# A graph kernel's attention stage: destination terms expanded in bfloat16 parts, with another order of the engines' work

## The reference, cut to what matters

```python
es = jnp.einsum('nhd,hd->nh', x, a_s)
ed = jnp.einsum('nhd,hd->nh', x, a_d)
logit = jax.nn.leaky_relu(es[src] + ed[dst], NEG_SLOPE)
logit = jnp.where(mask[:, None], logit, -1e+30)
mx = jax.ops.segment_max(logit, dst, num_segments=N)
p = jnp.exp(logit - mx[dst]) * mask[:, None]
den = jax.ops.segment_sum(p, dst, num_segments=N)
alpha = p / jnp.where(den > 0, den, 1.0)[dst]
msg = alpha[..., None] * x[src]
out = jax.ops.segment_sum(msg, dst, num_segments=N)
```

## Time and profile before

| | |
|---|---|
| median of 3 runs | 6694.62 us (6692.63 to 6696.04) |
| the profiled execution | 6689.12 us |
| its span | 6686.9 us |
| PE / DVE / ACT / POOL busy | 3841.0 / 3444.8 / 898.4 / 4148.2 us |
| attention stage | from about 1518 to 3014 us of the span |
| table made (L800, 16 copies) | 1508.33 to 1517.89 us |

### The profile page before, as it was taken

One profiled execution on the slowest core, in us unless ns is written; L12 is line 12 of the kernel. 1 busy time (PEld: TensorE's weight loads), 2 busy tenths in 40 slices (PEclk: granted clock), 3 DMA queues, 4 the chain that ended last, 5 costly groups with the idle time before them and its releaser, 6 DMA issues. The chain is left out here.

```text
span 6686.9 us, 101415 instructions
## 1 busy us (share of the span) xinstructions
PE 3841.0 (57%) x17939; PEld 2899.4 (43%) x17940; DVE 3444.8 (52%) x10929; ACT 898.4 (13%) x2786; POOL 4148.2 (62%) x3995
## 2 busy tenths in 40 slices
PE   0332222215666666662467777777677777777766
PEld 0221111115666666661434444444444444444446
DVE  4632222214444444448955665656566566556654
ACT  0210000000000000003331111111111111111111
POOL 3067777764444443434228888888888888888870
PEclk9855555555555555555688888888888888888888
DMA  1355555533333333332268788787778877787874
GB/s 49 117 137 145 142 145 145 145 83 97 95 96 96 97 97 96 95 89 101 50 181 169 165 170 169 165 170 167 168 165 169 170 167 169 169 167 166 171 151 127
DMA packets 917009, 908.21 MB, mean 136 GB/s; under 512 B 231003, under 2 KB 735099, under 8 KB 916759
## 3 DMA queue, kind: packets, MB, share of 16 engines
q0 software_dynamic: 238848, 434.00, 32.4%
q1 hardware_dynamic: 678119, 473.77, 26.3%
HBM read 656.68 MB, written 250.64 MB: 136 GB/s over the span
## 5 line engine op out<-in xcount | busy, mean ns | idle before, releaser
L1409 POOL DMA_INDIRECT sums<-msg_bsum,msg_sidx x928 | 1558.8, 1680 | 308.0 <-issue 268.9
L1551 PEld LDWEIGHTS msg_fwd_ps<-msg_onehot,msg_hid 128*128 128x128 f32 x3712 | 639.8, 224 | 1422.1 <-issue 1313.4
L1418 POOL DMA_INDIRECT msg_ga<-ab,msg_idx x928 | 951.4, 1025 | 390.7 <-issue 240.8
L851 POOL TENSOR_SCALAR att_keyhot<-k_ramp,att_keys 128x128 f32<-128x128 f32 x1028 | 602.3, 604 | 895.9 <-PE att_sum_ps L949 873.4
L1564 PE MATMUL msg_pre_ps<-msg_rw,msg_lt 128*128 128x512 f32 x1856 | 1110.2, 684 | 37.1 <-DVE msg_xs L1488 28.1
L1551 PE MATMUL msg_fwd_ps<-msg_onehot,msg_hid 128*128 128x64 f32 x3712 | 621.6, 298 | 819.0 <-DVE l_fwd L1470 814.3
L686 POOL DMA_INDIRECT max_xe<-rows,max_idx x832 | 800.1, 962 | 422.8 <-issue 253.3
L949 PE MATMUL att_sum_ps<-att_px,att_keyhot 128*128 128x136 f32 x2056 | 559.1, 454 | 537.4 <-DVE l_acc L895 521.5
L949 PEld LDWEIGHTS att_sum_ps<-att_px,att_keyhot 128*128 128x128 f32 x2056 | 478.3, 331 | 563.7 <-DVE l_acc L895 546.8
L1553 PE MATMUL msg_bwd_ps<-msg_hid,msg_same 128*128 128x256 f32 x1856 | 708.9, 469 | 0.0
L1522 ACT ACTIVATE msg_bsum<-msg_bwd_ps 128x256 f32<-128x256 f32 x928 | 356.2, 384 | 2564.5 <-PE msg_bwd_ps L1553 2550.1
(11 more groups left out here) (260 smaller groups left out, 4807.6 us busy)
## 6 DMA issues: line engine op xcount, KB each, us to landing
msg_rw<-ab SPq DMA_DIRECT2D x928, 128.0 KB
att_xe<-xe SPq DMA_DIRECT2D x1028, 72.0 KB, 2.5
att_keyrow<-key SPq DMA_DIRECT2D x257, 256.0 KB, 3.5
xe<-max_xe SPq DMA_DIRECT2D x104, 576.0 KB, 3.5
msg_lt<-in_efT SPq DMA_DIRECT2D x928, 32.0 KB
msg_ga<-ab,msg_idx POOLq DMA_INDIRECT x928
sums<-msg_bsum,msg_sidx POOLq DMA_INDIRECT x928
rows<-node_rows SPq DMA_DIRECT2D x50, 288.0 KB, 2.4
```

What stands on the lines that cost most here:

```text
L851: pool.tensor_scalar(keyhot[:, b, u, :], K.ramp[:, 1:P + 1], keys[:, b, u:u + 1], None, ALU.is_equal).then_inc(s_kh, 1)
L1409: pool.indirect_dma_start(T.sums[u % 2], bass.IndirectOffsetOnAxis(ap=sidx[:, b, u:u + 1], axis=0), bsum[:, b, u, :], None, compute_op=ALU ...
L1418: pool.indirect_dma_start(ga[:, b, u, :], None, T.ab, bass.IndirectOffsetOnAxis(ap=idx[:, b, u:u + 1], axis=0)).then_inc(s_ga[b], 16)
L1551: pe.matmul(fwd_ps[u % 2][:, q * WIN:(q + 1) * WIN], hid[:, b % 2, u, HID + q * P:HID + (q + 1) * P], onehot[:, b, u, :], start=True, stop ...
```

## The change

In words:

1. `node_maxima` writes the table as three bfloat16 parts: the term rounded to bfloat16, the rest rounded again, and the rest of that. A column of the table has 48 bfloat16 numbers. For each part there is a cast of all 3200 numbers of a partition, a subtraction (not after the last), and sixteen copies into the table, a buffer of its own now.
2. `expand` is a bfloat16 matmul with 48 columns. DVE's `select` has a first step more (step -1): a reduction that adds the three parts out of PSUM into `dv`; the other steps read `dv`.
3. `spread` is ACT's: `away` = |part + 1 - keyrow|, then `keyT` = relu(1 - away), in bfloat16. It comes last in ACT's tick, after `exponentials`. ACT also issues the `keyrow` transfer, into two slots for four.
4. PE does `expand(t-1)` before `sums(t-3)`. DVE does `add`, `weigh(t-3)`, and then the steps of `select(t-2)` with an `add` between.
5. `px` has two slots for four. `expand` waits for the reduction of two groups earlier and no longer for the argument.
6. The tables `reg_w` and `reg_e` of the second layer are loaded in `edge_inputs` for `lists`.

The core of the diff:

```diff
@@ node_maxima
-            for q, r in quads:
-                out, src = to_keys(q, r)
-                dve.tensor_copy(out, src).then_inc(s_keyed, 1)
-            dve.wait_ge(s_keyed, len(quads))
+            all4 = "p t r s h -> p (t r s h)"
+            rest = both[:, :, :, :, :].rearrange(all4)
+            for i in range(TERMS):
+                part = term[:, :, :, :, :].rearrange(all4)
+                if i:
+                    dve.wait_ge(s_keyed, i * len(quads))
+                L.link(dve.tensor_copy(part, rest))
+                if i < TERMS - 1:
+                    L.mark(dve.tensor_tensor(rest, rest, part, ALU.subtract))
+                for q, r in quads:
+                    out, src = to_keys(q, r, i)
+                    dve.tensor_copy(out, src).then_inc(s_keyed, 1)
+                L.wait()
+            dve.wait_ge(s_keyed, TERMS * len(quads))
@@ relation_attention
-        keyT = ph.sb("keyT", [P, RG, U * P])
+        away = ph.sb("away", [P, U * P])
+        keyT = ph.sb("keyT", [P, RG, U * P], BF16)
+        dv = ph.sb("dv", [P, U, S2])
-        px = ph.sb("px", [P, RG, U, XR])
-        dst_ps = [ph.ps(f"dst_ps{b}", [P, U, S2]) for b in range(2)]
+        px = ph.sb("px", [P, 2, U, XR])
+        dst_ps = [ph.ps(f"dst_ps{b}", [P, U, TERMS * S2]) for b in range(2)]
...
             def select(j, b, step):
-                if step == 0:
+                if step == -1:
                     dve.wait_ge(s_dst, j + 1)
+                    dve.tensor_reduce(dv[:, :, :], dst_ps[b % 2][:, :, :].rearrange("p u (t c) -> p u c t", t=TERMS),
+                                      AX.X, ALU.add).then_inc(s_sc, 1)
...
@@ DVE's tick
-                    if has(2) and u < 3:
-                        select(t - 2, slot(2), u)
-                    if has(3) and u == 2:
+                    if has(3) and u == 0:
                         weigh(t - 3, slot(3))
-                if has(1):
-                    spread(t - 1, slot(1))
+                    if has(2):
+                        select(t - 2, slot(2), u - 1)
...
@@ ACT
-            pipeline(act, GROUPS, RG, [(0, keep), (2, exponentials)])
+            def load(j, b):
+                if past(j, 2):
+                    act.wait_ge(s_away, j - 1)
+                    settle(act, K)
+                act.dma_start(keyrow[:, b % 2, :], key[ds(j, 1), :].to_broadcast([P, U * P])).then_inc(s_kr[b % 2], 16)
+
+            def spread(j, b):
+                act.wait_ge(s_kr[b % 2], filled(j, b, 2, 16) if isinstance(j, int) else (j - b % 2) * 8 + 16)
+                if past(j, 1):
+                    act.wait_ge(s_kT, j)
+                act.activation(away[:, :], keyrow[:, b % 2, :], ACT.Abs, bias=K.part1[:, 0:1], scale=-1.0).then_inc(s_away, 1)
+                if past(j, RG):
+                    act.wait_ge(s_dst, j - RG + 1)
+                act.wait_ge(s_away, j + 1)
+                act.activation(keyT[:, b, :], away[:, :], ACT.Relu, bias=K.ones[:, 0:1], scale=-1.0).then_inc(s_kT, 1)
+
+            pipeline(act, GROUPS, RG, [(0, load), (0, keep), (2, exponentials), (1, spread)])
@@ PE
-            pipeline(pe, GROUPS, RG, [(3, sums), (1, expand)])
+            pipeline(pe, GROUPS, RG, [(1, expand), (3, sums)])
```

More of the change, by code:

```diff
@@ L36 @@
 KC = -(-STEPS // P)
+TERMS = 3
 KKC = -(-KSTEPS // P)
@@ L764, in node_maxima @@
         both = ph.sb("both", [P, TILES, R, 2, H])
+        term = ph.sb("term", [P, TILES, R, 2, H], BF16)
         s_run, s_keyed = (ph.sem(n) for n in ("run", "keyed"))
@@ L768, in node_maxima, with to_keys @@
         quads = [(q, r) for q in range(KQ) for r in range(R)]
-        def to_keys(q, r):
-            out = K.edm[r * KWIN:(r + 1) * KWIN, :, :].rearrange("k (t q) c -> k t q c", q=KQ)[:, :, q, :]
-            return out, both[q * KWIN:(q + 1) * KWIN, :, r, :, :].rearrange("p t s h -> p t (s h)")
+        def to_keys(q, r, i):
+            out = K.edm[r * KWIN:(r + 1) * KWIN, :, i * S2:(i + 1) * S2].rearrange("k (t q) c -> k t q c", q=KQ)[:, :, q, :]
+            return out, term[q * KWIN:(q + 1) * KWIN, :, r, :, :].rearrange("p t s h -> p t (s h)")
         @block.gpsimd
@@ L818, in relation_attention @@
         p = ph.sb("p", [P, RG, U, H])
-        px = ph.sb("px", [P, RG, U, XR])
-        dst_ps = [ph.ps(f"dst_ps{b}", [P, U, S2]) for b in range(2)]
+        px = ph.sb("px", [P, 2, U, XR])
+        dst_ps = [ph.ps(f"dst_ps{b}", [P, U, TERMS * S2]) for b in range(2)]
         sum_ps = [[ph.ps(f"sum_ps{b}{q}", [P, 2, XR]) for q in range(U // 2)] for b in range(2)]
         s_xe = [ph.sem(f"xe{b}") for b in range(RG)]
-        s_kr = [ph.sem(f"kr{b}") for b in range(RG)]
-        s_key, s_kh, s_kT, s_dst, s_sc, s_arg, s_p, s_px, s_sum, s_acc = (
-            ph.sem(n) for n in ("key", "kh", "kT", "dst", "sc", "arg", "p", "px", "sum", "acc"))
+        s_kr = [ph.sem(f"kr{b}") for b in range(2)]
+        s_key, s_kh, s_away, s_kT, s_dst, s_sc, s_arg, s_p, s_px, s_sum, s_acc = (
+            ph.sem(n) for n in ("key", "kh", "away", "kT", "dst", "sc", "arg", "p", "px", "sum", "acc"))
         block = ph.block()
@@ L859, in _ @@
             windows = Windows(nc, dve, mybir.EngineType.DVE, K.reg_kw, KWINDOWS - 1, U, RG, 4)
[L861 to L865, removed]
             def select(j, b, step):
-                if step == 0:
+                if step == -1:
                     dve.wait_ge(s_dst, j + 1)
+                    dve.tensor_reduce(dv[:, :, :], dst_ps[b % 2][:, :, :].rearrange("p u (t c) -> p u c t", t=TERMS),
+                                      AX.X, ALU.add).then_inc(s_sc, 1)
+                elif step == 0:
@@ L870, in select @@
                     dve.wait_ge(s_xe[b], filled(j, b, RG, 16 * U))
-                    dve.tensor_tensor(logit[:, :, :], xe[:, b, :, XR:XW], dst_ps[b % 2][:, :, 0:H], ALU.add).then_inc(s_sc, 1)
+                    dve.wait_ge(s_sc, j * 3 + 1)
+                    dve.tensor_tensor(logit[:, :, :], xe[:, b, :, XR:XW], dv[:, :, 0:H], ALU.add).then_inc(s_sc, 1)
                 elif step == 1:
-                    dve.wait_ge(s_sc, j * 2 + 1)
+                    dve.wait_ge(s_sc, j * 3 + 2)
                     dve.scalar_tensor_tensor(leaky[:, :, :], logit[:, :, :], SLOPE0, logit[:, :, :], ALU.mult, ALU.max).then_inc(s_sc, 1)
@@ L1246, in edge_inputs @@
         ab_ps = [ph.ps(f"ab_ps{b}", [P, 2 * HID]) for b in range(2)]
-        s_w, s_x, s_sd, s_norm, s_h, s_hT, s_hTs, s_ab, s_abs = (
-            ph.sem(n) for n in ("w", "x", "sd", "norm", "h", "hT", "hTs", "ab", "abs"))
+        s_w, s_reg, s_x, s_sd, s_norm, s_h, s_hT, s_hTs, s_ab, s_abs = (
+            ph.sem(n) for n in ("w", "reg", "x", "sd", "norm", "h", "hT", "hTs", "ab", "abs"))
         s_st = [ph.sem(f"st{b}") for b in range(2)]
```

31 lines of the change are left out of this document (15 added, 16 removed).

## The result

The changed kernel took 6933.04 us (median of 4 runs, 6931.08 to 6940.59) beside 6693.62 us for the kernel before on the same chip: a ratio of 1.036, 95% interval 1.0342 to 1.0378. It is slower by 239 us; 197 was forecast, and 6933 lies in the stated range. The profiled execution took 6931.08 us, span 6929.0.

A forecast was written before the change was run, and what follows sets the result against it. PE and DVE taking turns, 5.80 us a tick, was taken as the bound. The new circle's terms sum to 6.44 us, +165 us over 257 groups; with +32 for the table, 6892 us, range 6790 to 6985, 8 in 10 within 6770 to 7010.

The forecast's parts named there:

- The mechanism: Attention stage: a whole DVE tick, then ACT, then PE, then the next DVE tick, one circle one tick long.
- The rival of the open circle: Attention stage: sums of t-3 don't wait for keyT of t-1; DVE's 2.8 us sets the tick, 5956 us; chance 0.02.
- a): PE to DVE: first sum matmul to first add takes 1.41 us, as before.
- b): DVE's tick, first add to end of argument: 2.59 us, with the reduction at 0.40 and the argument at 0.18.
- c): DVE to ACT: argument's end to exponential 0.11 us, exponential's start to ACT's next start 0.20; 0.31 in the tick.
- d): ACT: two keyT passes over 128x512 at 0.72 us each, 0.05 between them; 1.49 us, bounds 1.26 and 1.75.
- e): ACT to PE: keyT's end to the start of PE's expansion, 0.20 us.
- f): PE's expansion: four bfloat16 matmuls at 0.11 us each, 0.44 us for 1.73 before; bounds 0.20 and 0.87.
- The table: Making the table between last gather and barrier, DVE alone: 41.6 us for 9.6, +32 us; bounds +19 and +38.
- register work: PE's expansion: sequencer's address work exposed after the wait, 0.22 us a matmul, f 0.87, time 7002; chance 0.07.
- The clock: PE in the attention stage: expected to stay at 0.50; a rise to 2.4 GHz would give tick 5.79, 6724 us.
- what the new order hides: Attention stage: nothing but the second half of the sums, the keys and POOL's work runs beside the circle.

The follow-up runs named there:

- the two exchanges: Changed kernel with one order swapped: on ACT keyT's passes ahead of the exponential, 6207.0 us; or on PE the sums ahead of the expansion, 6336.05 us.
- both exchanges: Changed kernel with keyT's passes ahead of the exponential on ACT and the sums ahead of the expansion on PE: 6025.59 us, tick 3.08.
- fixed-address run: Changed kernel with fixed table columns in the expansion and no loading of window numbers by PE, exponential at scale 0: 6821.86 us, tick 6.20.
- one-comparison run: Changed kernel with one comparison a group on POOL for four, the other one-hot matrices staying zero: 6900.55 us, tick 6.52.
- parts-only run: Changed kernel's three bfloat16 parts with the order of the kernel before, keyT made by DVE: 6487.08 us, tick 4.89, ratio 0.9684 to the kernel before.
- order-only run: Changed kernel's order with the table in one float32 part, no casts or subtractions: 7114.21 us, tick 7.42, ratio 1.0622 to the kernel before.
- one float32 part and both exchanges: Changed kernel with ACT's and PE's orders both swapped and the table in one float32 part: 6185.37 us, tick 3.79.

## Why the prediction was right, point by point

**The mechanism** was right: one circle of a tick's length through DVE, ACT and PE, closed by ACT's order and by PE's. The waits show its three links, and the two exchanges undo it from either side. The rival of the open circle had it at 2.8 us a tick and 5956; opened by both exchanges, it is 3.08 and 6025.59.

**The sum.** Measured from add to add in the tick shown, against the prediction's terms:

| term | predicted | measured |
|---|---|---|
| a) sums to first add | 1.41 | 1.41 (2208.70 to 2210.11) |
| b) DVE's tick | 2.59 | 2.61 (2203.50 to 2206.11) |
| c) to exponential, to first pass | 0.31 | 0.18 (2206.11 to 2206.29) |
| d) two passes | 1.49 | 1.53 (2206.29 to 2207.82) |
| e) to PE | 0.20 | 0.24 (2207.82 to 2208.06) |
| f) expansion | 0.44 | 0.64 here, 0.72 one tick before |
| tick | 6.44 | 6.61 here, 6.67 on average |

The stage lost 0.88 us a tick, 225 us, where 165 was forecast. The table lost 22, where 32 was forecast, so 10 of the 60 us missed in the stage were made good there by luck. Together 247, which is what DVE's first rows of the next stage differ by (3014.34 and 3261.37); the stages behind it were 5 us shorter, and the span is 242 us longer.

**The term that was mis-sized is f.** It is 0.69 us on average for 0.44, and 0.25 us over 256 ticks is 64 us, where the stage's loss missed by 60. It was priced from matmuls in another stage without addresses to work out. The distance of 0.11 us between starts came near the measured 0.12 to 0.15 by luck: it was meant as the matmuls' own time, and the matmuls alone stand 0.04 us apart. The rival "register work" had the right cause and too high a price, 0.87 for 0.64 to 0.72. The fixed-address run shows both halves: 0.33 us for the matmuls and loads up to the first sum, about 0.36 for the sequencer, and 0.1 of e) beside it.

On the loads the Trainium skill, page "TensorE: Matmul & The Clock Gate", section "Weight-path perf modes", was nearer than the row: it says that weights which aren't float32 load in parallel chunks, and four loads took 0.21 us in that run, where float32 loads stand 0.22 us apart each. Its four times is a theoretical figure for 8-bit weights; the estimate made from it, that the 48 columns set the pace, agrees with the 0.04 us between starts, which is 48 columns at 1.2 GHz. Its 0.2 us for the expansion holds neither the time from the last matmul to the sums (0.21 us) nor the sequencer's, so by it the kernel's time would have been forecast 60 us further off.

**The term b) was right by luck, through two errors.** The reduction was 0.35 us long, inside its bounds, and held DVE for 0.26 of that (2204.35 to 2204.61), not 0.40; the argument took 0.33, not 0.18. The second was not foreseen: the one-comparison run puts it down to POOL's work beside it.

**The table** went as the Trainium skill, page "VectorE: DVE Perf Modes", section "Mode 4×_2P — both tricks at once", has it: its rule gave 0.4 us a copy and +22, the row's price +32; measured 0.39 and +22. The casts took 1.83 us and the subtractions 3.49, for 2.0 and 3.45. The upper bound of +38 was added up wrongly: casts at the subtraction's rate give +36.

**The clock** stayed at 0.50 in the stage, as forecast, and what the new order hides is what the prediction said: the second half of the sums, the keys and POOL's work.

## What to carry to other kernels

When engines take turns, write the order down as a circle with a length in ticks, and price each link; a queued instruction that waits for nothing itself inherits the wait of the one ahead of it. Here the same work took 6.67 or 3.08 us a tick, by the order of two pairs of calls. A link behind a wait also pays for its sequencer's address work: 0.47 us a tick here, and nothing visible in the parts-only run, where the sums were queued ahead of it. And try the two halves of a change apart: the parts were worth 209 us alone, and the order turned that into a loss of 239.

## What the runs showed of the hardware

- Address work of PE's sequencer in front of four matmuls, with nothing queued ahead, took 0.47 us a tick (6.67 with it, 6.20 without it and without the loading of window numbers). An address instruction is 46 ns in the trace; the matmuls' starts are 0.12 to 0.15 us apart with them exposed and 0.04 without.
- A DVE operation on two SBUF tensors of 128x32 (the argument) took 331 ns with POOL's comparisons running beside it and 185 ns without. The logit, of the same size and also beside POOL, took 186. In the order-only run it was the other way round: argument 181 ns, logit 267, leaky ReLU 330. What tells them apart stays open.
- POOL slows too: its comparison of 128x128 took 601 ns in the changed kernel. In the parts-only run three of four did as well, and the fourth, whose last stretch lies beside DVE's bfloat16 keyT, took 1.21 us, for a mean of 754. No run separates keyT from what else DVE does there.
- The granted clock did not follow the busy share: it stayed at 0.50 with PE 94% busy with one float32 part and both exchanges, and went between 0.50 and full, 0.60 on average, at 74% with the bfloat16 parts and the same order.
